# Moving the transfers of the attention's row maxima from the sync engine's queue to GpSimd's

## The reference, cut to what matters

```
q = heads(query @ Wq + bq) / scale
k = heads(key @ Wk + bk)
v = heads(value @ Wv + bv)
scores = jnp.einsum('bhqd,bhkd->bhqk', q, k)
scores = jnp.where(mask[:, None, None, :] == 0, NEG_INF, scores)
attn = jax.nn.softmax(scores, axis=-1)
ctx = jnp.einsum('bhqk,bhkd->bhqd', attn, v)
```

## Time and profile before

| | |
|---|---|
| median of 3 runs | 717.47 us (716.39 to 719.63) |
| the profiled execution | 720.1 us |
| its span, first to last instruction | 718.4 us |
| granted TensorE clock, mean | 0.976 |
| PE busy | 647.1 us (90%) |
| DVE busy | 421.0 us (59%) |
| ACT busy | 304.6 us (42%) |
| POOL busy | 263.6 us (37%) |

### The profile page before, as it was taken

One profiled execution on the slowest core, in us unless ns is written; L12 is line 12 of the kernel. 1 busy time (PEld: TensorE's weight loads), 2 busy tenths in 40 slices (PEclk: granted clock), 3 DMA queues, 4 the chain that ended last, 5 costly groups with the idle time before them and its releaser, 6 DMA issues.

```text
span 718.4 us, 14785 instructions
## 1 busy us (share of the span) xinstructions
PE 647.1 (90%) x5371; PEld 475.9 (66%) x5371; DVE 421.0 (59%) x1246; ACT 304.6 (42%) x624; POOL 263.6 (37%) x380
## 2 busy tenths in 40 slices
PE   7899998899989978779999999998999999992991
PEld 5465655677777766567565666657878888881881
DVE  6654757888889678842122122113668887773672
ACT  2323235777778815342222122220655555510560
POOL 4201102444444530044445654222111443345475
PEclk9999999999999999989999999999999999997897
DMA  8659844777774149942544983216313472122932
GB/s 277 194 154 212 219 94 97 118 122 123 122 126 88 33 144 95 364 152 46 133 95 82 315 234 62 48 22 179 117 39 133 158 254 88 68 82 75 330 137 78
DMA packets 100719, 98.92 MB, mean 138 GB/s; under 512 B 21878, under 2 KB 91001, under 8 KB 100644
## 3 DMA queue, kind: packets, MB, share of 16 engines
q1 hardware_dynamic: 91432, 81.52, 44.9%
q0 software_dynamic: 9216, 16.46, 10.3%
HBM read 60.15 MB, written 38.05 MB: 137 GB/s over the span
## 4 chain that ended last, share of the span: by engine, by line
PE 51%; DVE 4%; DMA 2%; issue 2%; POOL 1%; ACT 1%; POOLq 0%; SPq 0%; DVEq 0%; ACTq 0%
PE pc L1663 10%; PE pc L1640 8%; PE pc L2529 4%; PE pc L2229 4%; PE pc L2222 3%; PE pc L1020 3%; PE pc L2267 2%; PE pc L2220 2%; PE pc L1616 2%; PE pc L2189 1%; PE pc L1659 1%; PE pc L61 1%; PE pc L2297 1%; PE pc L2289 1%; PE pc L1628 1%
## 5 line engine op out<-in xcount | busy, mean ns | idle before, releaser
L494 DVE TENSOR_REDUCE neg_max<-pb_two 128x8 f32<-128x1024 f32 x64 | 78.1, 1220 | 15.6 <-PE pb_two L818 12.4
L659 ACT ACTIVATE probs<-pb_two,b_key_cols 128x1024 f32<-128x1024 f32 x64 | 76.9, 1202 | 21.2 <-PE pb_two L842 21.1
L1480 POOL DMA_INDIRECT scratch_resid<-y,k_idx x32 | 54.7, 1708 | 82.0 <-DVE y L1548 81.1
L1663 PE MATMUL pc<-w_dn,mid 128*128 128x256 f32 x320 | 73.3, 384 | 0.0
L1591 ACT ACTIVATE mid<-pc,b_up 128x512 f32<-128x512 f32 x35 | 24.1, 687 | 109.7 <-PE pc L1640 109.7
L1663 PEld LDWEIGHTS pc<-w_dn,mid 128*128 128x128 f32 x320 | 59.5, 190 | 12.7 <-issue 5.3
L1640 PE MATMUL pc<-gT,w_up 128*128 128x512 f32 x140 | 61.2, 592 | 0.0
L1548 DVE TENSOR_SCALAR y<-pc,gate 128x256 f32<-128x256 f32 x32 | 15.5, 484 | 65.5 <-PE pc L1663 47.3
L1471 POOL DMA_INDIRECT rows<-scratch_rows,k_idx x32 | 32.1, 1004 | 53.9 <-DVE k_idx L1322 38.4
L1640 PEld LDWEIGHTS pc<-gT,w_up 128*128 128x128 f32 x140 | 26.6, 190 | 30.5 <-issue 30.1
L369 POOL TENSOR_TENSOR v_wide<-v_all,s_zero 128x256 f32<-128x256 f32 x32 | 23.4, 730 | 47.8 <-PE pb L855 47.8
(11 more groups left out here) (376 smaller groups left out, 1433.5 us busy)
## 6 DMA issues: line engine op xcount, KB each, us to landing
qs<-scratch_qparts SPq DMA_DIRECT2D x48, 128.0 KB, 4.4
ks<-scratch_kparts SPq DMA_DIRECT2D x48, 128.0 KB
w_dn<-in_W_down SPq DMA_DIRECT2D x8, 640.0 KB
scratch_slots<-s_zero SPq DMA_DIRECT2D x1, 4160.0 KB, 20.0
cT<-in_ctxT SPq DMA_DIRECT2D x8, 512.0 KB, 5.9
s_x<-in_x SPq DMA_DIRECT2D x8, 512.0 KB, 6.8
scratch_rows<-s_x SPq DMA_DIRECT2D x16, 256.0 KB, 4.3
scratch_resid<-s_x SPq DMA_DIRECT2D x8, 512.0 KB, 7.3
```

Of the source, the lines that this page charges most:

```text
L494: V.tensor_reduce(neg_max[:].rearrange("p (b u j) -> p u b j", b=2, u=2)[:, u], ps_both[0][:].rearrange("p (b j k) -> p b j k", b=2, j=4), ...
L659: A.activation(probs[t % 2 * 2 + u][:], ps_both[1][:].rearrange("p (h q) -> p h q", h=HEADS // 2), ACT.Exp, bias=key_cols[:, 1, t:t + 1], ...
L1480: pool.indirect_dma_start(out=T["resid"], out_offset=bass.IndirectOffsetOnAxis(ap=S["idx"][:, e, c:c + 1], axis=0), in_=y[e % 2][:, c, :], ...
L1663: ins = nc.tensor.matmul(here(c), mid[e % 2][m][:, c * P:(c + 1) * P], w_dn[e % 2][:, m, :], start=False, stop=(m == MT - 2))
```

## The change

`move_max` goes from the sync engine's block into GpSimd's. Its two DMAs, their shape, target and semaphore stay; the issuing queue is another. In GpSimd's loop it stands between `add_bias(s)` and `split_max(s+3)`; for tiles 0 and 1 it stands behind their `split_max`. Where the sync engine had `move_max(s+2)` it now has, behind the block for s = 0 and ahead of the loads of the stacks, only the wait for `nmT` of tile s+2.

```diff
-            def move_max(t):
-                sp.wait_ge(nmT_s, t + 1)
-                for half in range(2):
-                    r = half * HALF + ROWS
-                    sp.dma_start(qs[t // QUAD % 3][r:r + 2, :, of_tile(t)],
-                                 nmT[t % 2][half * HEADS:(half + 1) * HEADS, :]).then_inc(nm_in[t % 2], 16)
...
                 store_keys(q)
-                if q == QUADS - 2:
-                    move_max(0)
                 store_queries(q)
...
             store_queries(QUADS - 1)
-            move_max(1)
             store_keys(QUADS - 1)
             for s in range(0, END):
-                if is_tile(s + 2):
-                    move_max(s + 2)
...
                 q = s // QUAD + 2
+                if is_tile(s + 2):
+                    sp.wait_ge(nmT_s, s + 3)
                 if q < QUADS:
...
+            def move_max(t):
+                pool.wait_ge(nmT_s, t + 1)
+                for half in range(2):
+                    r = half * HALF + ROWS
+                    pool.dma_start(qs[t // QUAD % 3][r:r + 2, :, of_tile(t)],
+                                   nmT[t % 2][half * HEADS:(half + 1) * HEADS, :]).then_inc(nm_in[t % 2], 16)
...
             for t in range(AHEAD):
                 split_max(t)
+                if t < 2:
+                    move_max(t)
             for s in range(0, END + 1):
                 if is_tile(s + 1):
                     widen(s + 1)
                 if is_tile(s):
                     add_bias(s)
+                if is_tile(s + 2):
+                    move_max(s + 2)
                 if is_tile(s + AHEAD):
                     split_max(s + AHEAD)
```

## The result

The changed kernel takes 738.23 us (median of 4 runs, 737.81 to 738.70) against 717.26 before (4 runs), ratio 1.028, 95% interval 1.025 to 1.031: 21 us slower. Forecast were 750, range 722 to 768. The profiled execution took 738.51 us with a span of 736.8; before they were 720.1 and 718.4. The direction and the loop that was named were right; but the loop is slower by only a third of what was forecast, and the rest of the 21 us comes from two things that the forecast had at nothing.

A forecast was written before the change was run, and what follows sets the result against it. It took a loop through GpSimd's two DMAs and TensorE's max_T and context to bound the attention: 27 x 5.53 = 149.3 us in place of 117.0, +32.3, +0.5 at the start, in all +33: 750 us, range 722 to 768.

The forecast's parts named there:

- the loop that was named: Attention: context, then POOL's widen, add_bias, two DMAs, split_max, then max_T and context again; period 5.53 us instead of 4.02.
- 3.27 + X: Period of the attention's closed loop: 3.27 us of other terms plus X, 5.53 us in the forecast.
- X: POOL's time for the two DMAs with gaps, between add_bias and split_max: taken as 2.26 us, range 1.3 to 2.9.
- the threshold of 0.75: Attention loop: the two DMAs with their gaps decide the period only where they take over 0.75 us of POOL.
- PE's waits for the DMAs are gone.: Attention: transfers have two periods, 11 us, to land, so PE no longer waits; gain of 8.4 us, already in the sum.
- Waits that stay with the DMA: Sign against the forecast: PE's waits in the attention still name the DMA; none for qs<-nmT was expected.
- Off SP: 0.: SP's queue: 64 issues of 0.61 us go, loads start up to 1.3 us earlier in a step; worth 0.
- Rival B: Attention: moved DMAs free to POOL but landing as late as before; time within 2 us of 717; chance 4%.
- Rival D: Attention: PE's granted clock falls, max_T and context take longer, +30 more, 780 us; with dearer DMAs, above 768, together 9%.

The follow-up runs named there:

- e1: Kernel before plus one GpSimd compute instruction (a power on 128x4) where the moved DMAs would stand, DMAs left on SP: 730.68 us, ratio 1.003.
- e12: Changed kernel with GpSimd moving only the second half of each tile's maxima and SP the first: 726.31 us, ratio 1.012.
- e10: Changed kernel without the stack loads of quads 3 to 7, later tiles computed from old stacks: 733.01 us, ratio 1.021.
- e4: Changed kernel with the second half of the key loads in a quad's fourth step instead of its third: 739.66 us, ratio 1.015.
- e13: Changed kernel again, unaltered, on the chip of the later group of runs: 737.47 us, ratio 1.028.
- e3: Changed kernel with move_max(s+2) behind split_max(s+3) instead of ahead of it: 757.48 us, ratio 1.040.
- e9: Kernel before plus a GpSimd compute instruction in the moved DMAs' place, SP waiting for add_bias(s) before issuing move_max(s+2): 724.76 us, ratio 1.008.
- e8: Kernel before plus 32 GpSimd DMAs in the projections, all landed before the attention's loop starts: 720.86 us, one run.
- e11: Kernel before without the stack loads of quads 3 to 7, later tiles computed from old stacks: 711.92 us, one run.

## Why the prediction was right, and where its steps were wrong

- **The loop.** Right. 3.27 + X gives 4.41 for the X of 1.07 read from the timeline to within 0.07, 4.26 for e1's 0.93 to within 0.06, and the threshold of 0.75 lies between e12 (open) and e1 (closed).
- **The size of X.** The mis-sized term. Taken were 0.85 us for each DMA and 0.56 for gaps; measured are 0.57 and none. The indirect DMAs of the earlier trace rows were the wrong neighbours: a plain DMA costs GpSimd 0.6 of one, and nothing between two. SP's 0.61 us was the nearer row. This term brings 27 x 0.39 = 10.5 us over the undisturbed 4.02, where the forecast had 27 x 1.51 = 40.8. The X of 1.07 lies below the forecast's own 1.3 to 2.9.
- **"PE's waits for the DMAs are gone."** Wrong, though they were given two periods of 5.53 us and got only 4.41. The 2.8 us to land were taken from GpSimd's gathers, in another stage (306 to 433 us, DMA share 0.59). Here the transfers take 3.6 in the median, and e10, with 1.8, shows that the stack loads make the difference. The 6.3 us that the view gives as the longest leaves out the worst case: tile 4's second transfer was issued by 127.03, and TensorE got the data at 137.35. The forecast booked -8.4 us here; 3.3 came on top instead. Waits that stay with the DMA were one of the forecast's own signs of being wrong.
- **"Off SP: 0."** Wrong, and not only by the 1.3 us a step that SP is freed of. The term left out that the transfers lost their place in the order. Before, SP issued the maxima of tile s+2 ahead of the loads of step s. Now SP needs only `nmT` for its loads, while GpSimd comes to the transfers behind `add_bias`. In the kernel before, for tile 4 (SP's queue, then TensorE's use of the data, without a wait):

```profile
125.10 1.29 SPq L259 DMA_DIRECT2D qs<-nmT  x2
126.43 3.05 SPq L242 DMA_DIRECT2D qs<-scratch_qparts  x3
```

```profile
130.58 0.40 PE L842 MATMUL pb_two<-qs,ks 51*128 51x128 bf16 x8
```

  In the changed kernel SP had issued all 14 stack loads of the first three steps between 120.07 and 127.08 us, twelve of them of 128 KB, and the transfers stand behind nearly all of them instead of behind seven (SP, GpSimd, TensorE):

```profile
123.72 1.26 SPq L242 DMA_DIRECT2D qs<-scratch_qparts  x3
125.03 1.38 SPq L251 DMA_DIRECT2D ks<-scratch_kparts  x3
126.45 0.63 SPq L252 DMA_DIRECT2D ks<-scratch_mask_row  x1
```

```profile
125.89 1.14 POOL L375 DMA_DIRECT2D qs<-nmT  x2
```

```profile
137.35 0.61 PE L843 MATMUL pb_two<-qs,ks 51*128 51x128 bf16 x8 [5.75 <-DMA qs<-nmT]
```

  e4 spreads the loads and brings the ratio from 1.028 to 1.015, some 9 us across two chips, and 7.8 us in the 27 periods of the profiles. Rival B's mechanism, the late landing, was real, beside the loop and not in its place.
- **The barrier.** Not foreseen: +5.1 us, a quarter of the loss. No row of before pointed to it, since the attention's block had no GpSimd DMA.
- **The clock.** Rival D was small but real. After TensorE's long wait at tile 4 its granted clock was 0.50, 1.2 GHz, for some us (stretch, busy times, clock, DMA, GB/s):

```profile
134.00:140.00 6.00, 2.65 (x49) 2.31 (x49) 1.53 (x4) 1.35 (x2) 0.00 (x0) 0.50 0.11 11
```

  The period behind that wait is 5.26 us instead of 4.41. From 150 to 250 us, in the loop, with TensorE idle 0.3 us a step, the granted clock was 1.00.

Of the 33 us forecast, a dear X gave 30 too many, and the stalls and the barrier take some 17 of them back (8.4 + 3.3 + 5.1). The total was near because the errors had opposite signs, and that is luck: with the measured period and nothing else, the sum would have been +2 us (27 x 4.41 = 119.1 in place of 117.0), some 720 us and outside the range of 722 to 768. What holds of the prediction is the direction, the loop and its threshold.

What stays open is why the transfers of tile 4 land so late. In the changed kernel SP's queue (`hardware_dynamic` in the view) kept all 16 DMA engines busy from 126.5 to 133 us, and GpSimd's (`software_dynamic`) moved no packet in that stretch, though both transfers had been issued by 127.03 (queue, packets, MB, share):

```profile
## 3 DMA queue, kind: packets, MB, share of 16 engines
q1 hardware_dynamic: 833, 0.75, 116.8%
```

Three readings fit: GpSimd's queue is passed over, its descriptors come late, or a transfer moves, on either queue, only when the loads issued ahead of it are through. The runs lean to the third. With nearly all 14 loads ahead of tile 4's transfers the wait is 5.8, 4.1 and 5.1 us (changed kernel, e13, e10), with nine or ten ahead 2.4 and 2.6 (e4, e12). (In e3 all 14 are ahead too, but TensorE came later itself and waited 1.5.) With seven ahead, on SP's queue, tile 4 has no wait, in the kernel before and in e9. In e4, GpSimd's queue moved tile 4's first packets between 128 and 129 us, while SP's still filled the engines, so it isn't shut out whenever they are full; in the changed kernel it moved none before 133. The run that would decide is missing: the changed kernel with SP's loads held back until GpSimd has issued.

## What to carry to other kernels

Before work is put on an engine that looks half idle, find where in its step the idle time lies, and add up the loop that runs through the chosen place: here an engine busy for 37% of the time had 0.79 us of room at that place. A small transfer that is needed two periods later was bound here by the big loads that lay beside it. Moving it to another queue didn't free it: the loads no longer had to wait their turn behind it, and went out ahead. So write down, for each queue, what stands ahead of the transfer before and after the move. Last, count what a queue leaves to pay at the end of its block.

## What the runs showed of the hardware

- A plain 4 KB DMA of 16 runs costs GpSimd 0.57 us of its own time, and two stand without a gap; SP's queue takes 0.61.
- At the end of this block GpSimd is idle for about 0.08 us longer for each DMA that it has issued there (1.5, 1.8, 4.0, 6.6 us for 0, 1, 32, 64), whether they landed 150 us ago (e8) or were issued over the whole loop (e12).
- For 6.5 us, while SP's queue filled all 16 DMA engines (116.8% by the packets' times), GpSimd's queue moved nothing; without the later loads its transfers land in 1.8 us in the median, with them in 3.6.
- The stack loads cost the kernel before 0.3 us a tile: its periods are 4.33 in the mean, and 4.02 without the later loads (e11). Its DMA share in this stage is 0.69.
